# Causal mask and running maximum of the scores in one VectorE instruction per head and query tile, with the softmax normalisation kept on the chip

## Chip, cores and metric

One core of one Trainium2 chip. The metric is the device time of one execution in microseconds; less is better. The engines are TensorE (PE, its weight loads PEld), VectorE (DVE), ScalarE (ACT), GpSimd (POOL) and SyncE (SP), which here only issues DMA transfers. Each runs its own instructions in order and waits on semaphores.

## What is computed

```python
def attn(x, w_qkv, b_qkv, w_out, b_out):          # B, T, C, H = 32, 257, 256, 16
    q, k, v = heads(split(x @ w_qkv + b_qkv))       # head width 16
    att = einsum('bhqd,bhkd->bhqk', q, k) / sqrt(16)
    att = where(causal, att, -inf)
    y = softmax(att) @ v
    return y.reshape(B, T, C) @ w_out + b_out

h = edges(x)                     # gray, two 3x3 Scharr filters, |.| summed, halved: 256 rows of 256
h = concat([cls_tok, h], axis=1) # 257 tokens
h = h + attn(layernorm(h), ...)
h = h + ffn(layernorm(h), ...)   # 8 bit fake quantisation, scale from max over the whole tensor
```

## The kernel before

Two stages. The first goes over the 32 images and leaves the residual `h2` of each in SBUF; the second (feed-forward, from about 1150 us on) isn't touched but for the names of two statistics. The first stage is a software pipeline: step `n` works on six images at once, `bW = n-1` (gray values through DRAM), `bC = n-2` (edge filters, first layer norm), `bP = n-3` (keys, queries, values), `bS = n-4` (scores and their maxima), `bT = n-5` (transposed scores, exponential, weighted values), `bO = n-6` (normalisation, output projection, second layer norm). Each engine has its own `step`, whose order is written out by hand; PE's stands at L1002 to L1035, DVE's at L726 to L795.

The causal row maximum is found first, so that the exponential can be taken of transposed scores. `scores(u)` (u = 0 to 7, two heads each) computes `q k` with queries on the partitions into the PSUM tile `SX`, 257 keys for the second query tile and 129 for the first, and adds the mask with a further matmul per head (L869: identity times `mask_s`, -1e30 above the diagonal) into the same accumulation. `maxima(u)` on DVE takes the negated maxima of both heads, one reduction per query tile (L668, L670), into `mneg`. `SX` has one buffer: `scores(u+1)` waits for `maxima(u)`. After four of them `turn_max` transposes eight heads' maxima on PE into `M[1]`, `split` on DVE cuts them in a bf16 high part and a bf16 rest (L679, L681), and SP's `max_rows` (L335) puts these as two more contraction rows of `qst`. `scores_t(u)` gives scores less maximum with keys on the partitions (`ST`), ACT takes the exponential (`prob`), POOL zeroes what lies above the diagonal (`select`), and `outputs(g)` multiplies by `vaug`, which has a column of ones after each head's 16 values, so that the denominators come out as row 16 of each group of 32 in `yun`.

The denominators go to DRAM (`den_dram`, L383), come back spread over 128 partitions (L397), DVE takes the reciprocals (L734), they go to DRAM again (L351) and are broadcast into `yn` (L359), and DVE multiplies (L741, 1024 columns). `project(t)` contracts the four groups of `yn`, half of whose rows are zero weights, with `wo_pad` (L985); the output bias is a row of `wo_pad`. `resid` (L762) adds `h2`; then come `stats`, `x2` (L786), `colmax` and the copies of the statistics (L791, L792).

SP issues in this order in a step: `max_rows(bT, 1)`, gray values, reciprocals, the next input image, broadcast of reciprocals, six `gst` loads for the edge filters, `max_rows(bS, 0)`, the last value row, six `kst` loads (L379), four denominator rows (L383), three `qst` loads (L389), the spread denominators (L397), three more `qst` loads. `scores(0)` of the next step waits for all six of `qst`.

## Time and profile before

| | us |
|---|---|
| median of 3 runs | 1469.43 (1462.7 to 1471.52) |
| profiled execution | 1472.33 |
| its span | 1470.6 |
| mean granted clock of TensorE | 0.869 of full speed |
| PE / DVE / ACT / POOL busy | 1096.2 / 933.9 / 660.3 / 508.6 |

A busy time says how long an engine had an instruction in work; a matmul's includes its way through the array, so neighbours overlap and only the distance of two starts tells what one costs in a row. In a timeline a row with x6 stands for six instructions merged; the bracket is the idle time before it and what ended it.

### The profile page before, as it was taken

What the parts mean: (1) busy time and instruction counts of PE and PEld (TensorE: products, weight loads), DVE (VectorE), ACT (ScalarE), POOL (GpSimd) and SP (SyncE); (2) the same over time, 40 slices, a digit from 0 to 9 for tenths busy, and PEclk for the clock granted to TensorE, in tenths of its full rate; (3) what the DMA queues carried; (4) which work ended last, traced back from release to release, by engine and by line L of the source; (5) the groups of instructions that cost most, each with busy time, mean ns of one, the idle gap of its engine ahead of it and who ended that gap; (6) DMA issues with size and microseconds to landing.
All of it is one profiled execution on the core that took longest, in us unless ns stands there. A gap on an engine that the chain in (4) does not pass through costs nothing. (4 is left out here: it accounts for less than half of the span.)

```text
span 1470.6 us, 28592 instructions
## 1 busy us (share of the span) xinstructions
PE 1096.2 (75%) x9702; PEld 749.7 (51%) x9702; DVE 933.9 (64%) x1955; ACT 660.3 (45%) x1107; POOL 508.6 (35%) x549
## 2 busy tenths in 40 slices
PE   2458888888878888888888788888766476755666
PEld 1236665665656666666656656666654233322332
DVE  1234666666666667565665765676647588888764
ACT  1235554454554444444444544554322476743332
POOL 5324444344454444444443443453320000002332
PEclk9978999999999898899989998999976699996655
DMA  3655454444554444454445545342420133411664
GB/s 88 164 128 129 123 133 113 126 132 120 139 145 111 125 125 124 118 144 126 120 115 121 136 117 142 102 111 75 125 56 16 39 140 135 176 60 35 201 235 151
DMA packets 157011, 177.21 MB, mean 121 GB/s; under 512 B 27897, under 2 KB 147614, under 8 KB 153886
## 3 DMA queue, kind: packets, MB, share of 16 engines
q1 hardware_dynamic: 156958, 176.52, 43.8%
q8 instruction: 31, 0.51, 0.2%
q14 instruction: 22, 0.18, 0.0%
HBM read 90.30 MB, written 35.16 MB: 85 GB/s over the span
## 5 line engine op out<-in xcount | busy, mean ns | idle before, releaser
L509 ACT ACTIVATE prob<-ST 128x772 f32<-128x772 f32 x256 | 209.1, 817 | 351.4 <-PE ST L883 347.4
L668 DVE TENSOR_REDUCE mneg<-SX 128x2 f32<-128x258 f32 x256 | 106.6, 416 | 203.5 <-PE SX L869 203.4
L866 PE MATMUL SX<-kst,qst 96*128 96x257 bf16 (+1 forms) x1024 | 169.0, 260 | 87.9 <-DMA qst<-qpart 48.8
L670 DVE TENSOR_REDUCE mneg<-SX 128x2 f32<-128x514 f32 x256 | 173.5, 678 | 0.0
L866 PEld LDWEIGHTS SX<-kst,qst 96*128 96x128 bf16 x1024 | 98.1, 103 | 144.6 <-issue 75.6
L883 PE MATMUL ST<-qst,kst 98*128 98x256 bf16 (+2 forms) x1536 | 149.2, 233 | 28.9 <-DMA qst<-mpart 28.0
L883 PEld LDWEIGHTS ST<-qst,kst 98*128 98x128 bf16 x1536 | 127.3, 104 | 52.0 <-DMA qst<-mpart 22.8
L869 PE MATMUL SX<-mask_s,ident_b 128*128 128x256 bf16 x512 | 148.5, 290 | 0.0
L444 POOL TENSOR_SCALAR_AFFINE_SELECT prob<-prob 128x1016 f32<-128x1016 f32 x128 | 144.9, 1132 | 0.0
L985 PE MATMUL M<-wo_pad,yn 128*128 128x256 f32 x512 | 139.0, 419 | 0.8 <-DVE yn L741 0.8
L900 PE MATMUL G<-prob,vaug 128*32 128x256 f32 (+2 forms) x3072 | 125.1, 295 | 4.6 <-POOL prob L444 4.6
L1456 PE MATMUL GU<-qst,hq 128*128 128x256 bf16 (+1 forms) x384 | 89.3, 386 | 48.7 <-ACT hq L1247 48.7
L442 POOL TENSOR_TENSOR tick<-half 128x2 f32<-128x2 f32 x128 | 27.1, 211 | 244.8 <-ACT prob L509 244.8
L920 PE MATMUL M<-gst,cw 102*32 102x256 f32 x1024 | 92.0, 491 | 24.7 <-DMA gst<-gray_dram 15.5
L985 PEld LDWEIGHTS M<-wo_pad,yn 128*128 128x128 f32 x512 | 101.2, 208 | 14.5 <-DVE yn L741 1.0
L900 PEld LDWEIGHTS G<-prob,vaug 128*32 128x32 f32 x3072 | 87.0, 116 | 40.4 <-issue 9.1
L454 POOL TENSOR_TENSOR kqr<-kqr,kpart 128x512 f32<-128x512 f32 x32 | 37.2, 1162 | 179.0 <-ACT kqr L521 179.0
L933 PE MATMUL M<-xT,wqkv 128*128 128x256 f32 x256 | 95.4, 508 | 0.0
L1413 PE MATMUL GU<-xqT,kpart 128*128 128x512 bf16 x192 | 58.7, 388 | 44.9 <-DVE hb L1320 20.0
L1456 PEld LDWEIGHTS GU<-qst,hq 128*128 128x128 bf16 (+1 forms) x384 | 42.0, 124 | 96.1 <-issue 55.7
L741 DVE TENSOR_TENSOR yn<-yun,yn 128x1024 f32<-128x1024 f32 x32 | 45.4, 1418 | 69.9 <-DMA yn<-rec_dram 69.8
L1226 ACT ACTIVATE silu<-GU,gsc 128x512 f32<-128x512 f32 x96 | 64.3, 683 | 40.7 <-DVE hb L1320 18.0
(220 smaller groups left out, 2011.5 us busy)
## 6 DMA issues: line engine op xcount, KB each, us to landing
kst<-kpart SPq DMA_DIRECT2D x192, 128.5 KB, 2.5
gst<-gray_dram SPq DMA_DIRECT2D x96, 256.0 KB
qst<-qpart SPq DMA_DIRECT2D x192, 128.0 KB, 2.4
yn<-rec_dram SPq DMA_DIRECT2D x128, 128.0 KB, 3.9
h_dram<-hb SPq DMA_DIRECT2D x12, 1280.0 KB, 4.6
hb<-h_dram SPq DMA_DIRECT2D x12, 1280.0 KB, 6.1
wg_raw<-in_x SPq DMA_DIRECT2D x48, 256.0 KB, 3.7
wu_raw<-in_x SPq DMA_DIRECT2D x48, 256.0 KB, 4.2
```

Of the source, the lines that this page charges most:

```text
L444: nc.gpsimd.affine_select(p, p, [[0, 4], [-1, 2], [1, P - 1]], ALU.is_ge, 0.0, base=1, channel_multiplier=-1).then_inc(sel_done, 1)
L509: nc.scalar.activation(prob[:, g % 2, 2 * (u % 2):2 * (u % 2) + 2, 0:QEND], ST[:, :, 0:QEND], ACT.Exp).then_inc(exp_done, 1)
L668: nc.vector.tensor_reduce(mneg[:, 0, 2 * u:2 * u + 2], SX[:, :, S0:S0 + P + 1], AX.X, ALU.max, negate=True)
L670: nc.vector.tensor_reduce(mneg[:, 1, 2 * u:2 * u + 2], SX[:, :, S1:S1 + T], AX.X, ALU.max, negate=True).then_inc(max_done, 1)
L866: mm(SX[:, r, at:at + k], qst[par][0:SR, 2 * u + r, P * t:P * t + P], kst[par][0:SR, 2 * u + r, 0:k], start=t == 1, stop=False)
L869: last = mm(o, ident_b[:, :], mask_s[:, :, :], start=False, stop=True)
L883: last = mm(ST[0:KEYS[k], r, QAT[k]:QAT[k] + QN[k]], kst[par_][:, i, KFIRST[k]:KFIRST[k] + KEYS[k]], qst[par_][:, i, Q0[k]:IMG], start=Tru ...
L900: last = mm(o, vaug[par_][0:KEYS[k], k, head_at(4 * g + j), :], prob[0:KEYS[k], g % 2, j, QAT[k]:QAT[k] + QN[k]], start=k == 0, stop=k == ...
L920: last = mm(M[1][32 * j:32 * j + 32, IMG * f:IMG * f + IMG], cw[:, f, :], gst[:, 4 * t + j, :], start=True, stop=True)
L933: last = mm(M[m][:, 0:IMG], wqkv[:, c, D + P * m:D + P * m + P], xT[:, c, 1:T], start=c == 0, stop=c == KC - 1)
L985: last = mm(M[0][:, D * t:D * t + D], yn[:, g, P * t:P * t + P], wo_pad[:, g, :], start=g == 0, stop=g == 3)
L1456: last = mm(GU[i][:, par, D * t:D * t + D], hq[par][0:IW[k], k, tok:tok + P], wdT[0:IW[k], k, :], start=k == 0, stop=k == IT - 1)
```

## The change

The score matmuls lose the mask matmul. `mask_s` becomes one row of 257 per partition: zeros for the first 129 columns, the triangle in the last 128, so that its last 129 or 257 columns serve either query tile. `maxima(u)` copies two elements (`seen`) and then runs four fused instructions, each: add the mask to a head's scores of one query tile, write the sum in bf16 to a scratch tile (`shown`), and leave the maximum in `mmax`. After the fourth group three small operations negate, round to bf16 and subtract, so that high part and rest stand side by side in `mneg`; `turn_max` transposes 16 columns instead of 8, and `split` is one copy.

The diff also changes the normalisation. The denominators go straight to 16 partitions of `den`, DVE takes 16 x 256 reciprocals, and a new PE part, `spread_rec`, multiplies them by a 0/1 table into `G`. Four SP transfers move every second group of `yun` into its free rows, so that `yn` and `wop` have two chunks in place of four and `project` half the matmuls. `yn` is computed between `maxima(1)` and `maxima(2)`. The output bias is added to `h2` when the edge row is stored (`bo_row`), the residual is summed in place in `h2`, its copy goes, and two small DVE operations go too (one to POOL, one because POOL writes `rstd2` itself).

```diff
@@ PE: scores(u)
                             for t, at, k in ((1, S1, T), (0, S0, P + 1)):
-                                mm(SX[:, r, at:at + k], qst[...][0:SR, 2 * u + r, P * t:P * t + P],
-                                   kst[par][0:SR, 2 * u + r, 0:k], start=t == 1, stop=False)
-                            o = SX[:, r, S1 + P + 1:S1 + P + 1 + 2 * SD].rearrange(...)[:, :, 0:P]
-                            last = mm(o, ident_b[:, :], mask_s[:, :, :], start=False, stop=True)
+                                last = mm(SX[:, r, at:at + k], qst[...], kst[...], start=True, stop=True)
@@ DVE: maxima(b, u)
-                    nc.vector.tensor_reduce(mneg[:, 0, 2 * u:2 * u + 2], SX[:, :, S0:S0 + P + 1], AX.X, ALU.max,
-                                            negate=True)
-                    nc.vector.tensor_reduce(mneg[:, 1, 2 * u:2 * u + 2], SX[:, :, S1:S1 + T], AX.X, ALU.max,
-                                            negate=True).then_inc(max_done, 1)
+                    nc.vector.tensor_copy(seen[:, u % 2, :], half[:, :])
+                    for r in range(2):
+                        i = 2 * (u % 4) + r
+                        for t, at, k in ((0, S0, P + 1), (1, S1, T)):
+                            last = nc.vector.tensor_tensor_reduce(
+                                shown[:, r, t, 0:k], SX[:, r, at:at + k], mask_s[:, T - k:T], 1.0, NEG,
+                                ALU.add, ALU.max, mmax[:, t, u // 4, i:i + 1])
+                    last.then_inc(max_done, 1)
+                    if u % 4 == 3:
+                        m = mneg[:, :, u // 4, 0, :]
+                        wait(dve, max_done, b, 8, u + 1)
+                        nc.vector.tensor_scalar(m, mmax[:, :, u // 4, :], -1.0, None, ALU.mult).then_inc(m_top, 1)
+                        wait(dve, m_top, b, 4, 2 * (u // 4) + 1)
+                        nc.vector.tensor_copy(mtop[:, u // 4, :, :], m).then_inc(m_top, 1)
+                        wait(dve, m_top, b, 4, 2 * (u // 4) + 2)
+                        nc.vector.tensor_tensor(mneg[:, :, u // 4, 1, :], m, mtop[:, u // 4, :, :], ALU.subtract
+                                                ).then_inc(m_low, 1)
@@ DVE: split(b, half_)
-                    nc.vector.tensor_copy(hi, M[1][0:H // 2, 0:IMG]).then_inc(msplit, 1)
-                    wait(dve, msplit, b, 4, 2 * half_ + 1)
-                    nc.vector.tensor_tensor(lo, M[1][0:H // 2, 0:IMG], hi, ALU.subtract).then_inc(msplit, 1)
+                    nc.vector.tensor_copy(mpart[half_][:, :], M[1][0:H, 0:IMG]).then_inc(msplit, 1)
@@ DVE: stats (bias: bo2 for bC, None for bO)
+                if bias is None:
+                    nc.vector.tensor_copy(passed[:, :], half[:, :])
...
-                nc.vector.tensor_scalar(h2[:, rows2(b), :], rows[:, :, :], 1.0, None, ALU.mult)
+                if bias is not None:
+                    nc.vector.tensor_tensor(h2[:, rows2(b), :], edge[:, :, :], bias, ALU.add)
+                else:
+                    nc.vector.tensor_copy(passed[:, :], half[:, :])
@@ DVE: step
                 maxima(bS, 0)
                 if valid(bO):
-                    wait(dve, den_loaded, bO, 16, 16)
+                    wait(dve, den_moved, bO, 64, 64)
                     nc.vector.reciprocal(den[:, :], den[:, :]).then_inc(rec_done, 1)
                 maxima(bS, 1)
+                if valid(bO):
+                    wait(dve, rec_spread, bO, 1, 1)
+                    wait(dve, y_moved, bO, 64, 64)
+                    wait(dve, out_done, bO - 1, 1, 1)
+                    nc.vector.tensor_tensor(yn[:, :, :], yun[:, 0:4:2, :], G[:, 1, :]..., ALU.mult).then_inc(yn_done, 1)
                 maxima(bS, 2)
-                if valid(bO):
-                    wait(dve, rden_loaded, bO, 64, 64)
-                    nc.vector.tensor_tensor(yn[:, :, :], yun[:, :, :], yn[:, :, :], ALU.mult).then_inc(yn_done, 1)
@@ PE: spread_rec, called between scores_t(bT, odd, 4) and outputs(bT, odd, 1)
+                        for c in range(KC):
+                            last = mm(G[:, 1, IMG * c:IMG * c + IMG], tab[0:H, C_SEL + P * c:C_SEL + P * c + P],
+                                      den[:, :], start=True, stop=True)
@@ PE: project(t)
-                        for g in range(4):
-                            last = mm(M[0][...], yn[:, g, P * t:P * t + P], wo_pad[:, g, :], ...)
+                        for c in range(KC):
+                            last = mm(M[0][...], yn[:, c, P * t:P * t + P], wop[:, c, :], ...)
@@ SP: step (rec_dram save and the four yn loads are gone)
-                        sp.dma_start(den_dram[j:j + 1], yun[32 * j + HD:32 * j + HD + 1, :, :]...)
+                        sp.dma_start(den[4 * j:4 * j + 4, :], yun[32 * j + HD:32 * j + HD + 1, :, :]...)
                 query_rows(range(0, 3))
                 if valid(bT):
-                    wait(sp, rec_saved, bT - 1, 16, 16)
-                    wait(sp, den_saved, bT, 64, 64)
-                    sp.dma_start(den[:, :], spread(den_dram)).then_inc(den_loaded, 16)
+                    wait(sp, den_moved, bT, 64, 64)
+                    for j in range(4):
+                        sp.dma_start(yun[32 * j + HD:32 * j + 2 * HD, 0:4:2, :], yun[32 * j:32 * j + HD, 1:4:2, :]...)
                 query_rows(range(3, 6))
```

## Rows read from the trace of the kernel before

**Rows 1.** The page, part 1: engine busy us (share of the span) xinstructions
```profile
PE 1096.2 (75%) x9702; PEld 749.7 (51%) x9702; DVE 933.9 (64%) x1955; ACT 660.3 (45%) x1107; POOL 508.6 (35%) x549
```

**Rows 2.** Busy time by window, twenty steps: window, length, engines, granted clock, DMA share, GB/s
```profile
237.90:879.50 641.60, 532.99 (x5438) 395.47 (x5439) 413.99 (x942) 307.49 (x540) 283.81 (x321) 0.92 0.50 126
```

**Rows 3.** Groups by line and shape: busy us, mean ns | idle us before
```profile
L869 PE MATMUL SX<-mask_s,ident_b 128*128 128x256 bf16 x512 | 148.5, 290 | 0.0
...
L734 DVE RECIPROCAL den<-den 128x32 f32<-128x32 f32 x32 | 10.8, 338 | 0.0
```

**Rows 4.** Timeline of one step, PE: start us, us, engine, line, operation, count [idle]
```profile
620.44 1.93 PE L920 MATMUL M<-gst,cw 102*32 102x256 f32 x16 [1.34 <-DVE mpart L681]
622.30 1.85 PE L933 MATMUL M<-xT,wqkv 128*128 128x256 f32 x4
...
626.97 0.27 PE L869 MATMUL SX<-mask_s,ident_b 128*128 128x256 bf16 x1
627.09 0.33 PE L866 MATMUL SX<-kst,qst 96*128 96x257 bf16 x2
...
628.80 1.07 PE L920 MATMUL M<-gst,cw 102*32 102x256 f32 x16
...
630.26 0.28 PE L869 MATMUL SX<-mask_s,ident_b 128*128 128x256 bf16 x1
...
640.56 1.99 PE L985 MATMUL M<-wo_pad,yn 128*128 128x256 f32 x8
...
650.45 0.33 PE L866 MATMUL SX<-kst,qst 96*128 96x257 bf16 x2 [1.42 <-DMA qst<-qpart]
...
651.73 1.08 PE L920 MATMUL M<-gst,cw 102*32 102x256 f32 x8
```

**Rows 5.** Timeline of the same step, DVE
```profile
631.00 1.22 DVE L741 TENSOR_TENSOR yn<-yun,yn 128x1024 f32<-128x1024 f32 x1 [2.40 <-DMA yn<-rec_dram]
632.14 0.42 DVE L668 TENSOR_REDUCE mneg<-SX 128x2 f32<-128x258 f32 x1
632.48 0.68 DVE L670 TENSOR_REDUCE mneg<-SX 128x2 f32<-128x514 f32 x1
...
635.07 0.43 DVE L689 TENSOR_SCALAR h<-edge 128x512 f32 x1 [0.15 <-DVE st L687]
...
636.32 0.41 DVE L681 TENSOR_TENSOR mpart<-M,mpart 8x256 bf16<-8x256 f32 x1
...
645.03 0.93 DVE L689 TENSOR_SCALAR h<-resid 128x512 f32 x1
...
648.53 0.72 DVE L786 TENSOR_SCALAR x<-resid,ag,rs 128x256 f32<-128x256 f32 x2
...
650.46 0.15 DVE L792 COPY stat<-rs 128x2 f32 x1
...
650.97 0.41 DVE L681 TENSOR_TENSOR mpart<-M,mpart 8x256 bf16<-8x256 f32 x1
```

**Rows 6.** Timeline of the same step, SP's queue: start of issue us, us of issue
```profile
636.76 1.33 SPq L335 DMA_DIRECT2D qst<-mpart  x2
...
642.90 1.25 SPq L383 DMA_DIRECT2D den_dram<-yun  x4
...
646.16 0.52 SPq L397 DMA_DIRECT2D den<-den_dram  x1
646.72 1.84 SPq L389 DMA_DIRECT2D qst<-qpart  x3
```

**Rows 7.** Waits over the whole span: us in total, times, longest us
```profile
DVE yn L741 <- DMA yn<-rec_dram: 69.8, 30, 7.4
...
PE SX L866 <- DMA qst<-qpart: 48.8, 26, 9.1
```

**Rows 8.** Two lines by source: duration ns min/median/max, first and last start us
```profile
L791 DVE COPY stat<-ag x32: 157/554/570, 171.8 to 1142.3; 128x2 f32 x22, 128x2 f32<-128x2 f32 x10
...
L757 DVE TENSOR_SCALAR xhat<-edge,ag,rs x64: 400/1231/1336, 55.4 to 1025.7; 128x256 f32<-128x256 f32 x64
```

164 lines of the change are left out of this document (88 added, 76 removed).

## The prediction, made before the changed kernel ran

> **What bounds the kernel now.** I read the page's engine row first: TensorE is busy three quarters of the span, VectorE two thirds [rows 1]. The page's chain that ended last covers under a quarter of the span and holds only lines of the second stage, so it says nothing about attention. I therefore measured attention by windows: twenty steps (from one `edges(0)` to the twentieth after it) take 641.6 us, 32.08 each, with PE busy 533.0, DVE 414.0 and a granted clock of 0.92 [rows 2]. No engine fills the stretch, so what counts is the order in which the engines hand work to one another. For that I walked one step, from `edges(0)` at 620.44 to the next one at 651.73, 31.29 us, and cut it where DVE ends the split of the first eight maxima (636.32 + 0.41 = 636.73) [rows 4, 5].
>
> First part, 16.29 us. PE runs without a gap to the end of `scores(3)` (630.26 + 0.28 = 630.54). DVE then doesn't start `maxima(3)`: ahead of it in its queue stands the `yn` product, which waited 2.40 us for the broadcast reciprocals and ran from 631.00. `maxima(3)` starts at 632.14, 1.60 after its scores. From there DVE alone sets the pace (maxima, layer norm statistics, split) [rows 4, 5]. The waits list says the same of the other images: 30 waits of `yn` for that DMA, 69.8 us, 2.3 each [rows 7].
>
> Second part, 15.00 us. The split releases SP at 636.76, and SP then issues one transfer behind the other; the last three `qst` loads are issued from 646.72 to 648.56. `scores(0)` starts at 650.45, after 1.42 us of waiting for exactly these, 1.89 after the last issue; `edges(0)` follows 1.28 later [rows 4, 6]. 26 images show that wait, 48.8 us in all, 9.1 of them one wait [rows 7]. Beside this SP chain runs a DVE chain that is hardly shorter: `resid`, `maxima(6)`, statistics, `maxima(7)`, `x2`, `colmax`, and the other split, which ends at 650.97 + 0.41 = 651.38 [rows 5]. It has 0.35 us of slack.
>
> **What the mask matmuls cost.** Their busy time is 148.5 us for 512 [rows 3], but a matmul's time includes its way through the array. Start to start one takes 0.12 (626.97 to 627.09) [rows 4], say 0.11: 56 us in all, 0.22 per `scores`. Of the eight `scores` of a step only those inside the first part (1 to 3) and `scores(0)` shorten a chain that decides.
>
> **What the new maxima cost.** Now a group takes 0.42 and 0.68 us for 258 and 514 columns; the second starts 0.34 after the first [rows 5]. So in sequence an operation costs 1.02 ns a column and 0.08 more: 0.95 for the pair. Four fused operations of 129 and 257 columns read the same 772 columns: 0.79 + 4 x 0.08 = 1.11. The copy of two elements ahead of them adds 0.07 to 0.155: L792, a copy of that size, lasts 0.15, and its follower starts 0.07 behind it [rows 5]. The trace has no fused add and max with a result of its own per partition; that result costs at least nothing, and at most a small operation of 0.155 for each. Counting 0.07 to 0.155 for it, four times 0.28 to 0.62, the group grows by 0.51 to 0.94. I take 0.70, between the two, because the result has to be written by someone but small operations overlap.
>
> The Trainium skill, page "VectorE: DVE Perf Modes", section "Two Vector instructions with no wait between them", says that an operation that also writes its accumulator is two instructions; no row here shows one. The same page, section "The DRAIN you can't avoid", says the next operation does not start until the pipeline is empty. The trace differs for reductions (the second starts 0.08 before the first ends [rows 5]), and by that rule the group would grow by 4 x 0.155 + 0.155 + 4 x 0.16 - 0.16 = 1.26.
>
> **First part, change by change.** Masks of `scores(1)` to `(3)`: 6 x 0.11 = -0.66. `spread_rec` puts four float32 matmuls ahead of `outputs(1)`; the projection's eight take 1.99 [rows 4], so +1.00. `yn` now waits for `rec_spread` behind `maxima(1)`, where DVE is idle for microseconds, is half as wide, and no longer stands before `maxima(3)`: 1.60 less a hand-over of 0.04 (SP follows the split by 0.03 [rows 5, 6]) gives -1.56. `maxima(3)`: +0.70. Three dependent small operations on `mneg`, at least 0.155 each: +0.50. The `h2` row becomes a two-input add: half of `yn`'s 1.22 and the fixed 0.08 make 0.69 instead of 0.43 [rows 5], +0.26. The split loses its second operation: -0.44. A small SBUF copy that meets a GpSimd operation waits for its end: L791, two elements, has a median of 0.554 and a minimum of 0.157, and L757 1.231 against 0.400 [rows 8]; GpSimd is busy 283.8 of 641.6 us [rows 2]. The copy in front of `maxima(3)` and the two small ones behind can meet this: 0 to 0.8, I take +0.25. Sum: **+0.05**, between -0.4 and +0.8. The reciprocal grows from 32 to 256 columns: (0.338 - 0.155) / 32 = 5.7 ns a column makes 1.6 us [rows 3]. It lies between `maxima(0)` and `maxima(1)`, while PE spends 3.7 us on `edges(0)` and `keys(0)` [rows 4]; if that cover were gone it would cost 1.3 a step. The small product moved to GpSimd is covered by that engine's idle time, over half of the stretch [rows 2]; uncovered it would cost one small operation.
>
> **Second part.** The load of `den` (0.52 and a gap of 0.04) goes; in its place, still ahead of the last three `qst` loads, SP issues four moves of `y`. Nearest rows: 0.31 each for the four single-row transfers L383, 0.61 for the `qst` loads [rows 6]. So 1.25 to 2.45, taken as 1.8: +1.2. `scores(0)` is 0.22 shorter before `edges(0)`. SP chain: **+0.98**, between +0.5 and +1.7. What SP no longer issues for the reciprocals (one save, four loads) lies before 636 and shortens nothing here. The DVE chain: projection halved -1.00, `maxima(6)` and `(7)` +1.40, the `h` copy (0.93 [rows 5]) replaced by two small copies -0.62, two other small copies gone -0.30, three `mneg` operations +0.50, split -0.44: -0.46. But `x2` (0.72 for its two [rows 5]) now comes about 1 us later behind its `maxima(7)`, and can meet a GpSimd operation there, at 1.23 instead of 0.40 each [rows 8]: up to +1.66. So -0.5 to +1.2, less the slack of 0.35: it stays below the SP chain or meets it.
>
> **Sum.** 31 steps x 0.05 = 1.5. The 26 steps whose `scores(0)` waited for `qst`: 26 x 0.98 = 25.5. In the other five the projection was late, and half of it gives back 1.0 each: -5. Together +22 us. Nothing in the second stage, 400 us, changes. The profiled execution took 1472.3 (span 1470.6), 2.9 above the median of 1469.4; the sum gives 1494 on it, and against the median about **1490 us**, 1.4% slower. About 1% (15 us) is what a measurement of this kernel can tell from no change.
>
> **Rivals.**
> - *VectorE becomes the bound.* If the fused operations cost their full duration, the group grows by 1.26: +0.56 in the first part, and in the second the DVE chain grows by -0.46 + 1.12 + 1.66 - 0.35 = 1.97, 0.99 over the SP chain. 31 x (0.56 + 0.99) = 48 more at worst, 1538; without the meeting of `x2` only the first part counts, 31 x 0.56 = 17 more, 1507. For it: DVE has 414 us of work in 641, and some 5 more per step brings it near 28 of 32. Against: the overlap in rows 5.
> - *Nothing to be seen.* The `y` moves issue in 0.31 each (+0.73) and the group grows by 0.51: first part -0.14, SP chain +0.5: +4 us in all, 1473.
> - *Faster, by the clock.* Behind the waits before it `edges(0)` runs at half rate: 16 matmuls in 1.93, against 1.07 at 628.80, and the four of `keys(0)` take 1.85 where 1.0 is usual [rows 4]. That is 1.7 us a step at the level of 1.2 GHz. If PE keeps 2.4 GHz there, 31 x 1.7 = 53 us come back: about 1440. From two steps in three on it makes the kernel faster by over 1%. Against: the wait in front gets longer, not shorter. The Trainium skill, "TensorE: Matmul & The Clock Gate", section "HAM oscillation — how this bites in real kernels", says that gaps bring the low clock; by it fewer matmuls mean more of it, and the trace agrees that the low stretch follows the idle one.
> - *Slower, by the clock.* One more low stretch in the first part costs as much: +50, 1540.
>
> **Chances.** Forecast 0.36 (of it 0.26 over 1% slower), VectorE the bound 0.18, slower by the clock 0.06, nothing 0.21, faster by the clock 0.19 (0.17 over 1%). Slower 0.50, same 0.33, faster 0.17. The range goes from 1445, short of the fast case, to 1530, inside the upper VectorE case.
>
> **What would show it.** After, `maxima(3)` should start within 0.2 us of its scores; a group of maxima should last about 1.7 us; the wait of `scores(0)` for `qst` should stay or grow, with four `y` moves between the two triples of loads; the step should be 32 to 33 us. A group over 2.2 us and a vanished `qst` wait mean the VectorE rival. A step under 31.6 with `edges(0)` at 1.07 means the clock. I am wrong altogether if `scores(1)` to `(3)` come to wait for DVE.

## The result, and the profile after

| | before | after |
|---|---|---|
| median, us | 1468.9 (1462.7 to 1471.5, 4 runs) | 1600.1 (1597.5 to 1602.4, 4 runs) |
| ratio, 95% interval | 1 | 1.0899 (1.0861 to 1.0938) |
| profiled execution, its span, us | 1472.3, 1470.6 | 1597.5, 1595.8 |
| mean granted clock over the span | 0.869 | 0.782 |

The change makes the kernel 131 us slower, nine per cent. The forecast was 22 us, and its range ended at 1530. All times here and below are medians of the fast runs of a kernel; norm_y_late, ttr_only and no_mask_mm had one slow run each, which is left out.

The page of the kernel after, its span and its engines' busy times (before: [rows 1]):

```profile
span 1595.8 us, 29250 instructions
...
PE 1107.0 (69%) x9062; PEld 725.9 (45%) x9062; DVE 1077.9 (68%) x3842; ACT 654.9 (41%) x1107; POOL 517.9 (32%) x580
```

There are 640 matmuls fewer (512 of the masks and 256 of the projection gone, 128 of `spread_rec` new), and yet TensorE is busy 11 us longer; VectorE has 144 us more. The windows of the kernel after, twenty steps and then the two parts of one step that answer to the step of [rows 4, 5] (columns as in [rows 2]; the third value from the end is the granted clock):

```profile
254.20:979.56 725.36, 548.85 (x5042) 384.71 (x5041) 508.83 (x2121) 303.95 (x540) 288.79 (x340) 0.78 0.38 100
621.16:638.72 17.56, 15.74 (x148) 10.56 (x146) 11.22 (x48) 10.01 (x18) 7.14 (x9) 0.84 0.39 108
638.72:657.49 18.77, 11.95 (x106) 8.94 (x106) 14.17 (x61) 5.23 (x9) 7.26 (x9) 0.72 0.35 93
```

A step takes 36.27 us in place of 32.08, and 31 times the difference of 4.2 is 130, the whole result. The last exponential ends 127 us later than before (1234 for 1107 us from the first instruction), and what follows it takes 362 us as it took 363. Both parts grew, the first from 16.29 to 17.56 and the second from 15.00 to 18.77. The granted clock of the twenty steps went from 0.92 to 0.78, and most of that is in the second part. The second part of the step of [rows 4, 5] in the kernel before, same columns:

```profile
636.73:651.73 15.00, 10.63 (x118) 8.56 (x118) 12.21 (x31) 5.22 (x9) 6.77 (x9) 0.98 0.40 108
```

It has 0.98 where the step shown now has 0.72. As means over 21 steps the second part went from 0.95 to 0.71 and the first from 0.89 to 0.86.

Where the second part went is in SP's queue of the same step (start of issue, us of issue; before: [rows 6]):

```profile
638.75 1.34 SPq L343 DMA_DIRECT2D qst<-mpart  x2
...
644.96 2.65 SPq L382 DMA_DIRECT2D den<-yun  x4
647.65 1.91 SPq L388 DMA_DIRECT2D qst<-qpart  x3
649.68 2.59 SPq L396 DMA_DIRECT2D yun<-yun  x4
652.32 1.88 SPq L388 DMA_DIRECT2D qst<-qpart  x3
```

The four denominator moves take 2.65 us where the four writes to DRAM took 1.25, and the four moves of `y` 2.59 where the load of `den` took 0.52. Together that is 3.47 us, and the issue of the last query load ends 15.45 us after the release by the split in place of 11.80. TensorE waits for it: from the waits of the kernel after (us in total, times, longest; before: 48.8, 26 [rows 7]):

```profile
PE SX L889 <- DMA qst<-qpart: 115.6, 32, 8.0
...
PE SX L889 <- DVE mmax L676: 92.4, 34, 3.9
```

The wait for the loads now comes in every image, and the one for the maxima has grown from 37.8 to 92.4 us. TensorE's timeline of the step (before: [rows 4]):

```profile
621.16 1.93 PE L942 MATMUL M<-gst,cw 102*32 102x256 f32 x16
623.02 2.08 PE L955 MATMUL M<-xT,wqkv 128*128 128x256 f32 x4
624.89 0.85 PE L889 MATMUL SX<-kst,qst 96*128 96x257 bf16 x4
...
626.35 1.27 PE L1003 MATMUL G<-den,tab 16*128 16x256 f32 x4
627.55 0.90 PE L923 MATMUL G<-prob,vaug 128*32 128x256 f32 x24
...
629.35 0.50 PE L889 MATMUL SX<-kst,qst 96*128 96x257 bf16 x4
...
639.96 0.51 PE L889 MATMUL SX<-kst,qst 96*128 96x257 bf16 x4 [2.95 <-DVE mmax L676]
...
642.05 1.57 PE L923 MATMUL G<-prob,vaug 128*32 128x256 f32 x24
643.55 2.07 PE L1015 MATMUL M<-wop,yn 128*128 128x256 f32 x4
...
656.08 0.81 PE L889 MATMUL SX<-kst,qst 96*128 96x257 bf16 x4 [3.23 <-DMA qst<-qpart]
```

From the end of the last issue (652.32 + 1.88) to `scores(0)` are 1.88 us, as before (1.89): the landing takes no longer, the issues do. `edges(0)` and `keys(0)` run at half rate as before. What is new is that the low level lasts longer: `scores(1)` at 624.89 takes 0.85 us for four matmuls, where the same four take 0.50 at 629.35. A second low stretch lies behind the wait for the maxima: the weighted values at 642.05 take 1.57 us where they take 0.90 at 627.55, and the halved projection takes 2.07 us for four matmuls where 1.99 served for eight [rows 4]. `spread_rec` holds up `outputs(1)` by 1.20 us from start to start. VectorE's timeline (before: [rows 5]):

```profile
634.59 1.63 DVE L773 TENSOR_TENSOR edge<-habs 128x512 f32<-128x512 f32 x1
...
638.31 0.41 DVE L695 CAST mpart<-M 16x256 bf16<-16x256 f32 x1
638.65 0.15 DVE L672 COPY seen<-half 128x2 f32<-128x2 f32 x1
638.72 0.28 DVE L676 CUSTOM_DVE_ANT_0 shown<-SX,mask_s 128x129 bf16<-128x129 f32 x1
638.93 0.07 DVE L676 DVE_READ_ACCUMULATOR2_ANT mmax<- 128x1 f32 x1
638.93 0.41 DVE L676 CUSTOM_DVE_ANT_0 shown<-SX,mask_s 128x257 bf16<-128x257 f32 x1
...
639.83 1.84 DVE L782 TENSOR_SCALAR xhat<-edge,ag,rs 128x256 f32<-128x256 f32 x2
...
652.36 1.72 DVE L809 TENSOR_SCALAR x<-h,ag,rstd 128x256 f32 x2
...
655.20 0.41 DVE L695 CAST mpart<-M 16x256 bf16<-16x256 f32 x1
```

A group of maxima takes 1.18 us from its start at 638.65 to the next operation at 639.83. The read of the accumulator is a record of its own, 0.07 to 0.08 us, and the next fused operation starts together with it, so it costs nothing. At the end of the step the two `x2` operations take 1.72 us where they took 0.72. GpSimd's timeline tells why:

```profile
652.67 1.26 POOL L488 TENSOR_TENSOR gray<-wu_raw 128x512 f32<-128x512 f32 x1 [2.22 <-ACT wu_raw L587]
654.00 1.26 POOL L490 TENSOR_TENSOR gray<-gray,wu_raw 128x512 f32<-128x512 f32 x1
```

The first `x2` operation takes 0.41 us; it started before GpSimd did. The second takes 1.39 us and ends at 654.08, just behind the first gray addition (652.67 + 1.26 = 653.93). The same meeting holds up the sum of `edge`, which now comes earlier in the step. By its source line (duration min/median/max; in the kernel before its mean is 823 ns in 250 to 900 us, now 1598):

```profile
L773 DVE TENSOR_TENSOR edge<-habs x32: 685/1623/1657, 51.3 to 1136.7; 128x512 f32<-128x512 f32 x32
```

In the kernel after, two kinds of step alternate in most of the stage, 36.3 and 35.3 us long (the first part 17.6 and 16.6), and the two `x2` operations take 1.8 us in the longer and 2.9 in the shorter. So how long `x2` is held up doesn't set the step there.

### The profile page after: what moved, and what is told of

It reads as the page before. It is cut to its first block and busy times, and to the rows that moved or that the text cites. A ratio compares the mean times of both kernels' runs of the same rounds, so it can differ in the third digit from the quotient of the medians.

```text
span 1595.8 us, 29250 instructions
## 1 busy us (share of the span) xinstructions
PE 1107.0 (69%) x9062; PEld 725.9 (45%) x9062; DVE 1077.9 (68%) x3842; ACT 654.9 (41%) x1107; POOL 517.9 (32%) x580
## 5 line engine op out<-in xcount | busy, mean ns | idle before, releaser
L889 PE MATMUL SX<-kst,qst 96*128 96x257 bf16 (+1 forms) x1024 | 161.2, 292 | 208.0 <-DMA qst<-qpart 115.6
L676 DVE CUSTOM_DVE_ANT_0 shown<-SX,mask_s 128x129 bf16<-128x129 f32 (+1 forms) x1024 | 303.1, 350 | 0.0
L672 DVE COPY seen<-half 128x2 f32<-128x2 f32 x256 | 45.8, 179 | 229.2 <-PE SX L889 229.1
L904 PE MATMUL ST<-qst,kst 98*128 98x256 bf16 (+2 forms) x1536 | 170.2, 253 | 28.9 <-DMA qst<-mpart 27.7
L923 PE MATMUL G<-prob,vaug 128*32 128x256 f32 (+2 forms) x3072 | 140.1, 319 | 2.3 <-POOL prob L443 2.2
L923 PEld LDWEIGHTS G<-prob,vaug 128*32 128x32 f32 x3072 | 95.1, 126 | 55.6 <-issue 28.8
L942 PE MATMUL M<-gst,cw 102*32 102x256 f32 x1024 | 96.1, 509 | 15.8 <-DMA gst<-gray_dram 15.1
L955 PE MATMUL M<-xT,wqkv 128*128 128x256 f32 x256 | 104.2, 548 | 0.0
L1015 PE MATMUL M<-wop,yn 128*128 128x256 f32 x256 | 100.5, 532 | 2.5
L787 DVE TENSOR_TENSOR h<-h,M 128x512 f32 (+1 forms) x32 | 22.0, 687 | 98.0 <-PE M L1015 98.0
L676 DVE DVE_READ_ACCUMULATOR2_ANT mmax<- 128x1 f32 x1024 | 79.8, 78 | 0.0
L955 PEld LDWEIGHTS M<-xT,wqkv 128*128 128x128 f32 x256 | 62.1, 268 | 33.5 <-issue 24.7
```

The lines of the kernel that those rows point to most:

```text
L676: last = nc.vector.tensor_tensor_reduce(shown[:, r, t, 0:k], SX[:, r, at:at + k], mask_s[:, T - k:T], 1.0, NEG, ALU.add, ALU.max, mmax[:, ...
L889: last = mm(SX[:, r, at:at + k], qst[par][0:SR, 2 * u + r, P * t:P * t + P], kst[par][0:SR, 2 * u + r, 0:k], start=True, stop=True)
L904: last = mm(ST[0:KEYS[k], r, QAT[k]:QAT[k] + QN[k]], kst[par_][:, i, KFIRST[k]:KFIRST[k] + KEYS[k]], qst[par_][:, i, Q0[k]:IMG], start=Tru ...
L923: last = mm(o, vaug[par_][0:KEYS[k], k, head_at(4 * g + j), :], prob[0:KEYS[k], g % 2, j, QAT[k]:QAT[k] + QN[k]], start=k == 0, stop=k == ...
L942: last = mm(M[1][32 * j:32 * j + 32, IMG * f:IMG * f + IMG], cw[:, f, :], gst[:, 4 * t + j, :], start=True, stop=True)
L955: last = mm(M[m][:, 0:IMG], wqkv[:, c, D + P * m:D + P * m + P], xT[:, c, 1:T], start=c == 0, stop=c == KC - 1)
```

## The experiments

Eighteen kernels ran, in groups on one chip each. The table gives times and ratios to the kernel before on the same chip, and for each profiled execution means over 21 steps, from the timelines: the step from `edges(0)` to `edges(0)`, its first part up to the end of split(0), the ends of the last query load's issue and of split(1) counted from `edges(0)`; then the mean duration of one `x2` operation and the granted clock, both in 250 to 900 us. Runs of one kernel lie up to 22 us apart (both_orders, 1553 to 1575, the profile is of the shortest), which is 0.7 us a step, and the first and last steps are not in the means: no_mask_mm has the longer step at the same time. Where step and time disagree, the time counts.

| kernel | us | ratio (95%) | step | first part | loads end | split(1) ends | x2 | clock |
|---|---|---|---|---|---|---|---|---|
| before | 1469 | 1 | 32.0 | 16.5 | 28.4 | 31.6 | 0.39 | 0.92 |
| after | 1600 | 1.090 (1.086 to 1.094) | 36.3 | 17.4 | 33.0 | 34.4 | 1.09 | 0.78 |
| mask_only | 1549 | 1.051 (1.045 to 1.058) | 35.0 | 18.1 | 30.0 | 34.9 | 0.88 | 0.82 |
| norm_only | 1620 | 1.101 (1.094 to 1.109) | 36.9 | 17.6 | 33.1 | 33.0 | 0.39 | 0.81 |
| before_4more | 1537 | 1.044 (1.037 to 1.051) | 34.1 | 15.7 | 30.3 | 30.4 | 0.39 | 0.85 |
| qst_first | 1537 | 1.044 (1.037 to 1.050) | 34.1 | 16.8 | 27.1 | 34.0 | 1.15 | 0.80 |
| norm_y_late | 1510 | 1.026 (1.018 to 1.034) | 32.7 | 16.3 | 29.3 | 32.2 | 0.39 | 0.86 |
| norm_qst_first | 1444 | 0.982 (0.977 to 0.986) | 30.7 | 15.9 | 26.2 | 30.7 | 0.39 | 0.93 |
| before_qst_first | 1467 | 0.997 (0.995 to 0.999) | 32.1 | 16.8 | 26.9 | 32.0 | 0.39 | 0.92 |
| no_mask_mm | 1470 | 0.997 (0.994 to 1.001) | 32.8 | 16.6 | 28.5 | 32.6 | 0.39 | 0.87 |
| ttr_only | 1556 | 1.052 (1.043 to 1.061) | 35.3 | 17.6 | 29.5 | 35.2 | 1.45 | 0.82 |
| mask_fill | 1577 | 1.070 (1.065 to 1.075) | 35.9 | 18.4 | 30.3 | 35.8 | 1.13 | 0.84 |
| no_mask_long | 1522 | 1.033 (1.028 to 1.038) | 34.2 | 17.1 | 29.0 | 34.1 | 0.85 | 0.85 |
| mask_gray_early | 1489 | 1.014 (1.009 to 1.020) | 32.6 | 17.7 | 29.6 | 32.3 | 0.41 | 0.84 |
| before_gray_early | 1459 | 0.991 (0.987 to 0.995) | 31.6 | 16.3 | 28.2 | 31.0 | 0.39 | 0.92 |
| mask_split_first | 1513 | 1.026 (1.021 to 1.032) | 33.7 | 18.1 | 30.0 | 33.0 | 0.43 | 0.84 |
| norm_both_orders | 1542 | 1.046 (1.040 to 1.051) | 35.0 | 20.4 | 30.7 | 34.7 | 1.34 | 0.84 |
| both_orders | 1568 | 1.067 (1.062 to 1.072) | 35.0 | 19.7 | 29.9 | 34.3 | 1.07 | 0.77 |
| after_gray_early | 1540 | 1.046 (1.043 to 1.049) | 34.3 | 18.6 | 28.8 | 34.2 | 0.41 | 0.78 |
| norm_gray_early | 1433 | 0.974 (0.970 to 0.979) | 30.7 | 15.0 | 25.3 | 30.7 | 0.39 | 0.89 |

My theory after the result: the growth of SP's queue makes the step longer, 3.5 us of it against 1.2 forecast. The rival: VectorE, by the fused maxima and what hangs on them, or TensorE's clock.

### The two halves of the change

**mask_only** is the kernel before with the mask part alone (the added line stands for the code shown with the change):

```diff
-    nc.vector.tensor_reduce(mneg[:, 0, ...], SX[:, :, S0:S0 + P + 1], AX.X, ALU.max, negate=True)
-    nc.vector.tensor_reduce(mneg[:, 1, ...], SX[:, :, S1:S1 + T], AX.X, ALU.max, negate=True)
+    seen, four tensor_tensor_reduce, and the three mneg operations of the change; no mask matmuls
```

> The kernel before with the mask part of the change alone: no mask matmuls, fused add and max, three small operations on mneg, one-copy split; the old normalisation through DRAM stays. Theory SP (the added time is the issue of SP's longer transfers ahead of the last qst loads): the group of maxima costs 0.25 more, the three small operations 0.6, the edge sum can meet GpSimd for 0.7, the split saves 0.44, the masks 0.9 a step, so 0.2 to 0.5 a step more, 1475 to 1490. Theory VectorE (the fused maxima make it slow): most of the 131 us are here, over 1560.

**norm_only** is the kernel after with the mask part undone, so with the sums, moves and `spread_rec` of the normalisation alone.

> The changed kernel with the mask part undone: mask matmuls, two reductions, two-operation split as before; normalisation on the chip, y moves and halved projection as after. Theory SP: the 3.6 us of additional issue ahead of the last qst loads stay, the wait of yn is gone, so 2.7 to 3.5 a step over before, 1555 to 1580. Theory VectorE: near or below before, at most 1490.

Measured: 1549 and 1620. My theory failed on both. The mask part, which leaves SP's queue as it was (28.4 and 30.0 us, later only as the first part is), costs 80 us by itself, and the normalisation part costs 151 alone and 51 on top of the mask part. So the two don't add up: each of them has a chain of its own to the end of the step, and the later one counts. With the mask part alone split(1) ends 0.1 us before `edges(0)`; with the normalisation alone `edges(0)` waits for the query loads.

### SP's queue

**before_4more** adds four transfers of the shape of the `y` moves to the kernel before (left out here: it waits for the four of the step before):

```diff
     sp.dma_start(den[:, :], spread(den_dram)).then_inc(den_loaded, 16)
+    for j in range(4):
+        sp.dma_start(spare[32 * j:32 * j + HD, :, :], wqkv[32 * j:32 * j + HD, :, 2 * D:2 * D + P])
```

> The kernel before with four more transfers of the shape of the y moves (16 partitions, two pieces each, of 512 bytes, a constant into a scratch tile that nobody reads) issued between the two triples of qst loads; nothing else. Theory SP: four issues of 0.65 put 2.6 us on every step whose scores(0) waits for qst, +65 to +80, 1535 to 1550. If SP's issue is hidden: within 5 us of before.

**qst_first** is the kernel after with the loads ahead of the moves:

```diff
-    den moves (den[4 * j:4 * j + 4] <- yun)
-    query_rows(range(0, 3))
-    y moves (yun <- yun)
-    query_rows(range(3, 6))
+    query_rows(range(0, 6))
+    den moves
+    y moves, in the next step, behind max_rows(bT, 1)
```

> The changed kernel with only the order of SP's transfers altered: all six qst loads go right behind the kst loads, the four den moves behind them, and the four y moves at the start of the next step behind max_rows. Theory SP: scores(0) no longer waits for qst; then VectorE's chain, whose split ended 1.9 us before the next edges(0), sets the step: 1.8 us a step less, 1535 to 1550, and less if TensorE's clock rises with the shorter wait. Theory VectorE: 1590 to 1600, no change.

Both came out as the theory of the queue had it: +67 us and -63 us. SP's queue of before_4more, same columns as above:

```profile
647.79 0.51 SPq L399 DMA_DIRECT2D den<-den_dram  x1
648.43 2.59 SPq L402 DMA_DIRECT2D spare<-wqkv  x4
651.06 1.88 SPq L391 DMA_DIRECT2D qst<-qpart  x3
```

The four moves issue in 2.59 us, exactly as in the kernel after, though their rows are half as long (two of 512 bytes on each of 16 partitions). Nothing reads them, and `scores(0)` starts 1.9 us after the last issue ends, as in the kernel before, so it is their issue time in the queue that costs 67 us.

**norm_y_late** and **norm_qst_first** take the moves out from between the loads one after the other, in the normalisation part: first only `y`, then the denominators' moves too.

> The normalisation part alone (1620 us) with the four moves of y at the start of the next step, the denominator moves left where they are. Theory A (the terms as the rows of after show them: den moves 2.65 against 1.25 us of before, y moves 2.59 against 0.52, so 2.6 of the 4 us between the loads go with y): 1525 to 1545 us, and a last step from here to 1444 by the den moves. Theory B (the prediction's sum: the den moves cost what they did before, all of the growth is y): 1440 to 1460 us.

> The normalisation part alone (1620 us), with the six query loads ahead of the four denominator moves and the four moves of y put at the start of the next step. Theory A (the queue of SP sets the end, as in the changed kernel, where the same order took 63 us off): 1540 to 1560 us. Theory B (without the fused maxima, VectorE's chain ends earlier too, so the whole 5.3 us between the denominators' moves and the last query load comes off): 1470 to 1510 us.

Measured: 1620, 1510, 1444. The moves of `y` are worth 110 us and those of the denominators 67. The three kernels ran on three chips, and the runs of norm_y_late go from 1502 to 1515, so the split between the two is good to some ten microseconds; by the ratios it is 111 and 65. By issue time each set would be 31 x 2.6 = 82, so about half and half. The two together save 176 us, 14 more than their issue time, and the granted clock climbs from 0.81 to 0.86 and 0.93 alongside; that the clock is what adds the rest is likely and not shown. The prediction's sum had nothing at all for the denominators. And norm_qst_first is 1.8% faster than the kernel before (1.4 to 2.3%): once its transfers are out of the way, the normalisation part is a gain.

**before_qst_first** is the same order in the kernel before, den_dram writes and the load of `den` behind the six loads.

> The kernel before with the six query loads ahead of the den_dram writes and of the load of den; nothing else. Theory A (before, SP's queue set the end of the step in part: its last load ended at 28.37 us, 2 us before scores(0)): 0.5 to 1 us a step come off, 1440 to 1460 us, so most of the 30 us that the normalisation part with that order gains is the order's. Theory B (VectorE's end of the step is as late as the queue): 1465 to 1480 us.

Measured: 1467, ratio 0.997 (0.995 to 0.999). The loads end 1.5 us earlier and the step stays at 32.1, since split(1) ends at 32.0. So of the gain of norm_qst_first the order alone gives nearly nothing. In that kernel split(1) ends at 30.7. What it has besides the order is that the broadcast of the reciprocals is gone, for which VectorE waited 2.3 us on average with each `yn` [rows 7], and half of the projection; which of the two makes the gain was not tested.

### What the mask part costs

**no_mask_mm** is the kernel before without the mask matmuls:

```diff
-    o = SX[:, r, ...]
-    last = mm(o, ident_b[:, :], mask_s[:, :, :], start=False, stop=True)
```

(The two score matmuls then start and stop an accumulation each.)

> The kernel before with the sixteen mask matmuls of a step left out and nothing else: the maxima keep their two reductions and now run over keys of the future too, which only makes them larger. A step loses 16 x 290 ns = 4.6 us of TensorE work, 0.88 us of it on the path by the prediction's own count (0.66 in the first part, 0.22 in scores(0)). Theory A (the work left out is time saved, the clock does not care): 1440 to 1450 us and a granted clock near 0.92 in the stretch 250 to 900 us. Theory B (with less work between the same waits TensorE is granted a lower clock, and the slower matmuls give the saving back or more): 1465 to 1510 us, with a clock under 0.87 in that stretch and sc3 (the end of scores(3) after edges(0)) not earlier than the 10.01 us of before.

Measured: 1470, ratio 0.997 (0.994 to 1.001), with this window (columns as before):

```profile
250.00:900.00 650.00, 521.00 (x5102) 378.62 (x5100) 401.36 (x929) 302.28 (x535) 279.89 (x318) 0.87 0.49 123
```

Sixteen matmuls a step gone, and no time gained. The 4.6 us of the expectation are busy time, which includes the way through the array; at 0.12 us from start to start [rows 4] they are 1.9. `scores(3)` ends 9.34 us after `edges(0)` on average in place of 10.12 (10.01 is where the last query-key matmul ends, without the mask matmul behind it). That is 0.78 for the 0.66 of the prediction, but it is a mean over steps that differ by more than 2 us: where TensorE is at full clock from `edges(0)` on, 8.52 becomes 8.18, and in the slower steps most often seen 10.15 becomes 9.48. `maxima(3)` stands behind `yn` [rows 5], and its wait behind `scores(3)` grows from 1.8 to 2.8 us, so nothing of this reaches it. The granted clock falls from 0.92 to 0.87. Work taken from an engine that waits anyway is not time.

**ttr_only** leaves the fused maxima and takes two of the three small operations away, **mask_fill** gives TensorE its columns back:

```diff
 ttr_only
-    mtop and the subtraction ahead of turn_max
+    the bf16 copy and the subtraction in split, as before
 mask_fill, per head, behind the four score matmuls
+    for t in range(QT):
+        last = mm(SX[:, r, S0 + P + 1:512], qst[par][0:SR, ...], kst[par][0:SR, 2 * u + r, 0:511 - S0 - P], ...)
```

> The mask part alone (1549 us) with the maxima split into their two bf16 pieces after the transposition, as before, in place of ahead of it: of the three small operations ahead of turn_max only the negation stays, and the subtraction after it comes back (0.41 us twice a step). Theory A (the three small operations, held up by GpSimd, carry a large part): the way from the last maximum of a half to turn_max falls from 1.7 us to 0.3, and the time to 1505 to 1530 us. Theory B (the fused maxima themselves and the clock carry it): 1540 to 1560 us.

> The mask part alone (1549 us), with two matmuls of 126 columns per head written into the unused columns of SX after each pair of score matmuls, about the columns that the mask matmul had; nothing reads them. Theory A (VectorE and its small operations make the 80 us of the mask part): the time stays or grows by what the fillers cost, 1545 to 1585 us. Theory B (the lower clock makes most of it): the granted clock in 250 to 900 us comes back from 0.82 to 0.88 or more and the time falls to 1500 to 1530 us.

Measured: 1556 and 1577, neither better than 1549. The fillers raise the clock only from 0.82 to 0.84, with `x2` at 1.13 us in place of 0.88. Windows from 250 to 900 us, mask_only and then mask_fill:

```profile
250.00:900.00 650.00, 505.94 (x4754) 369.25 (x4755) 466.38 (x1981) 282.57 (x503) 254.97 (x297) 0.82 0.45 116
```

```profile
250.00:900.00 650.00, 519.90 (x5237) 391.28 (x5236) 473.38 (x1935) 278.21 (x491) 245.26 (x288) 0.84 0.44 114
```

So the 80 us don't come back with TensorE's missing work. That is not a proof that the clock has no part in them: no run brought it back to 0.92 with the fused maxima in place. The length of the small operations isn't the cause either: in ttr_only turn_max(1) comes 1.2 us earlier (30.7 for 31.9) and split(1) ends 0.3 later, because each `x2` takes 1.45 us in place of 0.88 and the split has its second operation back (0.4).

**no_mask_long** tests the length of a group alone:

```diff
+    nc.vector.tensor_reduce(spare[:, u:u + 1], SX[:, 0, 0:192], AX.X, ALU.max)
     nc.vector.tensor_reduce(mneg[:, 0, 2 * u:2 * u + 2], SX[:, :, S0:S0 + P + 1], ...)
```

> The kernel before without the mask matmuls (1472 us), with one more reduction ahead of the two in each group of maxima: over 192 columns of one head's scores, into a spare column that nobody reads. By the two reductions seen (258 columns in 0.416 us, 514 in 0.677) it adds about 0.28 us to a group, which is what the fused maxima and the copy ahead of them add (1.19 + 0.09 against 0.94 + 0.07 from the start of a group to the next operation). Theory A (the length of a group is what the mask part costs, whatever the instructions in it are: TensorE waits for every group before it may write SX again): 1530 to 1560 us, as the mask part alone (1549). Theory B (it is the kind of the new instructions: small copies held up by GpSimd, the read of the accumulator): at most 1500 us.

Measured: 1522, between the two theories: 52 of the 79 us between no_mask_mm and mask_only come with 0.28 us more in each group, with the old instructions. But the kernel's `x2` takes 0.85 us too. Each slow kernel of this row has that mark, so the length may act only by bringing `x2` to the gray additions. In mask_only, VectorE and GpSimd at the end of a step:

```profile
660.87 0.17 DVE L682 TENSOR_SCALAR mneg<-mmax 128x16 f32<-128x16 f32 x1
661.08 1.21 DVE L684 CAST mtop<-mneg 128x16 bf16<-128x16 f32 x1
662.33 0.18 DVE L686 TENSOR_TENSOR mneg<-mneg,mtop 128x16 f32<-128x16 f32 x1
662.42 1.68 DVE L799 TENSOR_SCALAR x<-resid,ag,rs 128x256 f32<-128x256 f32 x2
...
664.98 0.41 DVE L694 CAST mpart<-M 16x256 bf16<-16x256 f32 x1
```

```profile
661.01 1.26 POOL L487 TENSOR_TENSOR gray<-wg_raw 128x512 f32<-128x512 f32 x1 [1.80 <-ACT wg_raw L586]
662.34 1.29 POOL L489 TENSOR_TENSOR gray<-gray,wg_raw 128x512 f32<-128x512 f32 x1
```

The conversion to `mtop`, 16 columns that take 0.17 us elsewhere, takes 1.21 and ends as the first gray addition does; `x2` then meets the second: 1.68 us for the pair, which took 0.72 before.

**mask_gray_early** moves the gray scalings on ScalarE ahead of exponential(bS, 0) and the additions on GpSimd ahead of select(bS, 0), and leaves VectorE's order as it is. **before_gray_early** does the same in the kernel before.

> The mask part alone (1549 us), with ScalarE's three gray scalings put ahead of its exponential(bS, 0) and GpSimd's two gray additions ahead of select(bS, 0), into stretches where both engines wait; VectorE's order is as it was. Theory A (the mask part pushes x2 into the gray additions, and x2 held up sets edges(0)): x2 falls from 0.88 to 0.39 us each, the three operations ahead of turn_max(1) from 1.7 to 0.6 us, and the time to 1485 to 1510 us. Theory B (the longer groups alone do it): 1530 us or more.

> The kernel before with the gray scalings and additions early and nothing else. Its x2 operations take 0.39 us, so if the 60 us of the mask part were the collision, this stays within 1 per cent of before, 1458 to 1480 us. If moving them were a gain by itself, of 20 us or more, it comes out under 1450 us.

Measured: 1489 and 1459. Of the 80 us of the mask part 60 go (55 by the ratios), where the same move gives 12 in a kernel whose `x2` is not held up. The durations of `x2` by source line (min/median/max), mask_only and then mask_gray_early:

```profile
L799 DVE TENSOR_SCALAR x<-resid,ag,rs x64: 400/408/1366, 170.9 to 1219.9; 128x256 f32<-128x256 f32 x64
```

```profile
L799 DVE TENSOR_SCALAR x<-resid,ag,rs x64: 405/408/414, 167.5 to 1155.0; 128x256 f32<-128x256 f32 x64
```

The maximum falls from 1366 to 414. The collision is shown: it is worth the difference, between 40 and 50 us. What is left, 1489 against 1459, no run takes apart: the longer groups and small copies are in it, `seen` meets the moved additions now (0.33 us for 0.23), and the granted clock is 0.84 against 0.92.

### The end of VectorE's step

**mask_split_first**, **norm_both_orders** and **both_orders** put split(1) ahead of `x2`, in mask_only, norm_qst_first and qst_first:

```diff
     maxima(bS, 7)
+    split(bS, 1)
     x2, colmax, mean
-    split(bT, 1)      # at the start of the next step
```

> The mask part alone (1549 us), with split(1) moved from the start of the next step to right behind maxima(7), ahead of the two x2 operations, the column maxima and the two small copies. Theory A (VectorE's chain at the end of the step, from the last maximum over x2 to split(1), sets edges(0)): 1.5 to 2 us a step come off, 1490 to 1510 us. Theory B (the groups of maxima set every round and the end of the chain is only one of several that end together): at least 1530 us.

> The normalisation part alone with the query loads first (1444 us so far) and split(1) ahead of x2. Theory A (the end of VectorE's chain sets edges(0), which starts 0.05 us after split(1) in that kernel): 1 to 2 us a step come off, 1385 to 1415 us. Theory B (TensorE has no more than that to give): 1430 to 1445 us.

> The changed kernel with the six query loads ahead of the moves (1537 us so far) and split(1) ahead of x2 too. Theory A (with the loads early, VectorE's end of the step, 3.6 us from turn_max(1) to split(1), sets edges(0)): 2 us a step come off, 1465 to 1485 us, about the kernel before. Theory B (the groups of maxima and TensorE's clock hold the step): 1510 us or more.

Measured: -36, +98 and +31 us. I had expected a gain in all three. Split(1) does end sooner behind turn_max(1), but `x2` now starts 0.9 to 1.4 us later, and stands ahead of `maxima(0)` where split(1) stood. In mask_only this takes it past the gray additions (0.88 becomes 0.43). In norm_qst_first it takes it into them (0.39 becomes 1.34), and `maxima(0)`, queued behind, starts 3.3 us after `edges(0)` in place of 0.1 before it. A step of norm_both_orders, whose `edges(0)` starts at 581.92:

```profile
581.79 2.54 DVE L795 TENSOR_SCALAR x<-h,ag,rstd 128x256 f32 x2
...
585.37 0.41 DVE L668 TENSOR_REDUCE mneg<-SX 128x2 f32<-128x258 f32 x1
```

```profile
586.45 0.34 PE L875 MATMUL SX<-kst,qst 96*128 96x257 bf16 x2 [2.40 <-DVE mneg L670]
```

`scores(1)` waits 2.40 us for these maxima, and TensorE runs at half rate behind that wait (the weighted values at 590.16 take 1.57 us for 0.90): `scores(3)` ends 15.1 us after `edges(0)` in place of 10.6. In both_orders `x2` is held up in either order (1.15, then 1.07 us), so its duration doesn't explain the 31 us; what changed is that it now stands ahead of `maxima(0)`. One reordering, two signs: it gained where `x2` was free at its new place and lost where it was held up there.

### The whole change, repaired

**after_gray_early** has the loads first and the gray operations early. **norm_gray_early** has both without the mask part.

> The changed kernel with the query loads first (1537 us) and the gray scalings and additions early. Theory A (x2 beside the gray additions, 1.15 us each in place of 0.39, is the second cause in the whole change as in the mask part alone): 1470 to 1490 us, what is left being the longer groups of maxima. Theory B (in the whole change the groups and the clock weigh more): 1505 us or more.

> The normalisation part with the query loads first (1444 us), and the gray scalings and additions early as well. x2 takes 0.39 us there already. Theory A (the gray additions cost only where they meet x2): 1435 to 1450 us. Theory B (they also hold up maxima and the denominators' reciprocal at the start of the step): 1400 to 1430 us.

Measured: 1540 and 1433. norm_gray_early is the fastest kernel of this study, 2.6% below the kernel before. It is 11 us under norm_qst_first, with `x2` the same in both; they ran on different chips and their intervals overlap, so that difference isn't certain. In after_gray_early `x2` fell from 1.15 to 0.41 us and nothing was gained (1537 before): my second cause doesn't carry over to the whole change. The gain shows in the second part, and the first takes it back: from split(0) to split(1) it is 15.6 us in place of 17.2, and the first part is 18.6 in place of 16.8. One collision is left in it: the sum of `edge` still meets GpSimd's subtraction and takes 1.61 us, where it takes 0.68 in norm_gray_early. Its steps come in turns of three, about 32.1, 33.4 and 37.0 us, with a first part of 16.6, 17.5 and 21.1. The first 15 us of a short and of a long step (columns as before; the clock is the third value from the end):

```profile
523.00:538.00 15.00, 14.76 (x146) 10.04 (x146) 10.14 (x43) 8.59 (x17) 6.79 (x8) 0.89 0.50 133
588.50:603.50 15.00, 15.00 (x98) 9.60 (x99) 5.93 (x28) 5.18 (x11) 4.36 (x6) 0.57 0.29 79
```

The same chain of matmuls, at 0.89 and at 0.57. TensorE is busy throughout both. In the short step the rate doubles behind `keys(0)`:

```profile
526.56 0.50 PE L888 MATMUL SX<-kst,qst 96*128 96x257 bf16 x4
...
529.23 1.13 PE L954 MATMUL M<-xT,wqkv 128*128 128x256 f32 x4
```

In the long one it stays low for nine microseconds more:

```profile
592.24 0.85 PE L888 MATMUL SX<-kst,qst 96*128 96x257 bf16 x4
...
597.20 2.07 PE L954 MATMUL M<-xT,wqkv 128*128 128x256 f32 x4
```

`scores(3)` starts 10.0 and 10.9 us after `edges(0)` in the two shorter kinds and 14.5 in the long one. In front of both `edges(0)` shown (523.00 and 588.50) TensorE had stood idle for 0.80 us. Over 21 steps TensorE's idle stretches of more than 0.3 us in the 16 us ahead of `edges(0)` add up to 6.1 to 7.0 us in front of a long step and to 5.6 to 6.2 in front of the others, so they overlap, and no run separates a cause. For the whole change this stays open: why its clock is 0.78 and stays there once `x2` and the query loads are out of the way. That the low stretches take the time of the long steps is shown by these rows; that they would be gone with a shorter wait is not.

## Why the prediction was wrong, point by point

**What bounds the kernel** was read rightly. The two chains at the end of a step, SP's and VectorE's, are the ones that decide. The slack of VectorE's that I read as 0.35 is 0.4 as a mean (split(1) ends at 31.6 of 32.0). It is no reserve for a gain on SP's side: with the loads 1.5 us earlier, in before_qst_first, split(1) ends at 32.0 and the step stays.

**The masks**: -0.66 in the first part, and -0.78 as a mean in no_mask_mm, with -0.34 and -0.67 in steps of like clock. That these lie around the forecast is partly luck, since the clock moves the same figure by 2 us. It gained no time. In `scores(0)` it can't be seen beside the clock.

**The maxima**: +0.70 a group, measured +0.24 (1.18 against 0.94). The prediction took most of a small operation for each accumulator, which costs nothing. The rival with 1.26 rested on the Trainium skill's "The DRAIN you can't avoid" ("VectorE: DVE Perf Modes"), and the trace doesn't agree for fused operations: the second starts 0.21 us into the first one's 0.28. The same page's other section, that an operation with an accumulator is two instructions, is what the rows show. The rival that VectorE becomes the bound hung on this term; it came out at a third of the forecast, and VectorE's chain became the bound in the mask part all the same, by `x2`.

**First part**: forecast +0.05, measured +0.95 (16.46 to 17.41, means over 21 steps). `spread_rec` 1.2 for 1.0; hand-over to `maxima(3)` 1.81 to 0.04 us, so -1.77 for -1.56; the small operations on `mneg` 0.59 for 0.50; `h2` 0.69 as forecast; reciprocal 1.74 for 1.6, covered. Two terms are missing. `maxima(3)` comes earlier, and with it the `edge` sum, into GpSimd's subtraction for `kpart`: 0.78 more a step. The prediction let only small copies meet GpSimd in the first part, not the sum of two tensors. And `scores(3)` ends 1.19 later after `edges(0)` (10.12 to 11.31), of which `spread_rec` at 1.20 less the masks at 0.66 explain 0.54; behind the rest stands the low clock, which lasts past `scores(1)`.

**SP's queue**: the step that failed worst. The place was right and the size a third of what came. That the denominators' moves would cost what they had was never written down as a term: L383 stood in [rows 6] at 0.31 us an issue, and the change gives it another destination, four partitions of SBUF in place of a row of DRAM. It measures 0.66. The moves of `y` were bounded by 1.25 and 2.45 and taken at 1.8; they measure 2.59, above even the upper bound, which came from the nearest shape, the `qst` loads at 0.61 each. +3.47 in all for +1.2. By norm_y_late and norm_qst_first the unpriced half weighs 67 us of kernel time in the normalisation part and the other 110. In the whole change the two together weigh 63 (qst_first).

The Trainium skill says under "Issuing engines are not separate DMA queues" ("DMA: Bandwidth & Descriptors") that the sequencer's time to start a DMA is usually small beside the DMA. By it four more issues would be nothing here. The runs differ: four more issues a step cost 67 us of kernel in before_4more, because on this queue a load stands behind the issue times of all in front of it, 0.65 us each here.

**VectorE's chain**: the meeting of `x2` with GpSimd was in the prediction, at +1.66 a step, and it measures 2 x (1.09 - 0.39) = 1.4. The chain as a whole was to grow by -0.5 to +1.2; from split(0) to split(1) it grew from 15.2 to 17.0, by 1.8. The term "projection halved -1.00" is the one that didn't come: in the second part four matmuls at half rate take 2.07 us in all 21 steps, where eight took 2.24 on average, so it is -0.17. The sentence after it, "it stays below the SP chain or meets it", held in the kernel after only because SP's queue had grown by still more (split(1) ends 1.9 us before `edges(0)`). Once the loads are early (qst_first), or in the mask part alone, where SP's queue is unchanged, this chain sets the step, and mask_gray_early gives over half of the cost of the mask part back. The Trainium skill has the rule, in "Who interferes with whom" of "SBUF — State Buffer": VectorE's copies, conversions and operations with a scalar in their faster modes, and those with two inputs in SBUF, share ports with GpSimd, and the one that comes second waits for the whole of the other. The traces agree: in the kernel after `x2`, `seen` and `edge` are held up, to 1.48, 1.14 and 1.66 us, and `mtop` to 1.21 in the step of mask_only; the reciprocal (1.730 to 1.741), the reductions, the fused maxima (0.275 to 0.424) and `h` with its input in PSUM never are.

**The clock**: "slower by the clock", with +50 us and 6 in 100, and "faster by the clock" with 19. The window of twenty steps fell from 0.92 to 0.78, the low stretch at `edges(0)` reached past `scores(1)`, and the second part of the step fell from 0.95 to 0.71. The Trainium skill's "HAM oscillation" section, named in the prediction, has it that waits bring the low clock; the trace agrees in direction, the wait of `scores(0)` having grown from 48.8 to 115.6 us. Its price in the kernel after isn't separated by any run. Of the two signs I gave the wrong one three times the chance, although the forecast itself made the wait longer.

**The sum**: 31 x (0.95 + 3.28) = 131 us is what the steps show and what the kernel lost; 31 x 0.05 + 26 x 0.98 - 5 was the forecast. Of what was to be looked for, `maxima(3)` within 0.2 us of its scores came (0.04) and the wait for `qst` grew; the group was to be 1.7 us long and is 1.2, the step was to be 32 to 33 and is 36.3. Slower was forecast with 50 in 100 and came, but by terms of another size. Of the 131 us, 63 go with the order of SP's queue; of the other 68 it is known that they come with the mask part, which costs 93 on top of norm_qst_first (1444 to 1537), and no run takes them apart.

## What to carry to other kernels

Price every transfer whose source or destination changes as a new one, at its issue time, and count the issue times between a release and the load that somebody waits for: here four small ones cost 67 us. Where two chains end within half a microsecond of each other, growth of either lengthens the step, and a repair of one gained nothing here while the other stayed. Before moving any VectorE operation on SBUF data, look for the GpSimd operations that run at its new place: the same reordering gave -36 us where `x2` ran free at its new place, and +98 and +31 where it was held up there.

## What the hardware showed that was not expected

- One issue of a small transfer on SP takes 0.65 us with SBUF on both ends (16 partitions to 16, or one row to four partitions), and 0.31 from one row of SBUF to DRAM [rows 6].
- A fused add and max with a result per partition costs what a reduction of its columns costs, 0.21 us for 129 columns and 0.35 for 257 from start to start; its accumulator read of 0.08 us runs beside the next one.
- A VectorE copy of two elements per partition can take 1.14 us, beside a GpSimd operation.
- TensorE at full busyness was granted 0.57 of its clock over 15 us in one step of three (after_gray_early), and 0.89 and 0.82 in the other two, with the same instructions; the two steps shown had the same 0.80 us of idle time in front.
- Half of a projection's matmuls at half rate took as long as all of them had: 2.07 us for four, against 1.99 for eight in the step of [rows 4].
